# First two 256-row slots of a mixture-of-experts kernel joined into one of 512 rows

## The reference

```
h = rmsnorm(layernorm(x)) * gamma
q, kv, a = split(h @ w_qkva.T);  a = sigmoid(a)
y[n] = a[n] * y[n-1] + kv[n]            # scan along the 1024 rows of a batch
x = x + q * y
z = layernorm(x)
logits = z @ router_w.T                 # 7 experts, the best 2 taken
combine = softmax over the 2 best logits, placed at their experts
x = x + sum_e combine_e * swiglu_e(z) + swiglu_shared(z)
swiglu(z) = (silu(z @ wg) * (z @ wu)) @ wd        # 256 -> 1024 -> 256
```

## Time and profile before

| | us |
|---|---|
| median of 3 runs (982.82 to 985.39) | 982.82 |
| the profiled execution's own time | 982.58 |
| its span | 980.8 |
| PE busy in the span | 972.9 (99%) |
| DVE busy | 587.6 (60%) |
| ACT busy | 477.4 (49%) |
| POOL busy | 395.3 (40%) |

### The profile page before, as it was taken

How to read it: one execution, slowest core, us unless ns; L and a number is a source line. 1 busy time by engine, 2 the same in 40 slices (tenths; PEclk the granted TensorE clock), 3 DMA queues, 4 the chain that set the end, 5 groups by cost and what they waited for, 6 DMA issues and landing times.

```text
span 980.8 us, 15883 instructions
## 1 busy us (share of the span) xinstructions
PE 972.9 (99%) x5565; PEld 849.2 (87%) x5565; DVE 587.6 (60%) x1043; ACT 477.4 (49%) x769; POOL 395.3 (40%) x265
## 2 busy tenths in 40 slices
PE   8999999999999999999999999999999999999998
PEld 6888998888889998888888888888888999999887
DVE  7988687787653134455445544654464455646677
ACT  5565434323422324456545544554465466767564
POOL 3336100000021243464645554655556488776300
PEclk9999999999999999999999999999999999999999
DMA  9433300000049995544463456345535576775393
GB/s 320 120 87 86 87 22 22 16 8 22 1 139 356 326 297 181 199 123 145 166 207 102 158 175 202 94 164 183 189 89 176 188 266 209 267 240 166 89 331 107
DMA packets 146034, 155.06 MB, mean 158 GB/s; under 512 B 75449, under 2 KB 134338, under 8 KB 138818
## 3 DMA queue, kind: packets, MB, share of 16 engines
q1 hardware_dynamic: 139248, 136.08, 42.8%
q0 software_dynamic: 6720, 18.36, 6.0%
q10 hardware_dynamic: 18, 0.01, 0.0%
HBM read 127.67 MB, written 26.74 MB: 157 GB/s over the span
## 4 chain that ended last, share of the span: by engine, by line
PE 93%; DVE 4%; ACT 1%; issue 1%; POOL 0%; DVEq 0%; POOLq 0%; ACTq 0%
PE ps L1158 40%; PE ps L1136 15%; PE ps L1114 11%; PE ps L1139 8%; PE ps L1020 6%; PE ps L1204 4%; PE ps L1181 4%; PE ps L1212 2%; PE ps L1002 1%; PE ps L1031 1%; DVE h_lo L1767 1%; PE ps L983 1%; DVE h_early L1761 1%; ACT h_hi L886 1%; DVE y_sb L1354 0%
## 5 line engine op out<-in xcount | busy, mean ns | idle before, releaser
L1158 PE MATMUL ps<-xs_hi,w_both 128*128 128x512 f32 x1216 | 380.4, 391 | 0.1
L1158 PEld LDWEIGHTS ps<-xs_hi,w_both 128*128 128x128 f32 x1216 | 228.3, 188 | 49.0 <-DVE ps L1761 0.9
L652 POOL TENSOR_TENSOR w_both<-w_raw,w_both 128x2048 fp32r<-128x2048 f32 x45 | 223.5, 4966 | 107.1 <-ACT w_both L823 98.5
L1158 PE MATMUL ps<-xs_lo,w_both 128*128 128x512 f32 x608 | 236.7, 389 | 0.0
L1136 PE MATMUL ps<-w_both,h_hi 128*128 128x512 f32 x656 | 233.0, 398 | 0.1
L1139 PE MATMUL ps<-w_both,h_lo 128*128 128x256 f32 x656 | 184.1, 281 | 0.0
L1767 DVE TENSOR_TENSOR h_lo<-ps,h_hi 128x512 fp32r<-128x512 f32 x152 | 105.1, 691 | 103.1 <-ACT h_hi L886 81.7
L676 POOL DMA_INDIRECT x_stage<-z_rows,idx_x x70 | 72.3, 1032 | 224.8 <-DVE idx_x L1673 160.8
L1761 DVE TENSOR_TENSOR ps<-ps,silu 128x512 f32<-128x512 f32 x152 | 106.2, 699 | 90.8 <-ACT silu L879 62.2
L879 ACT ACTIVATE silu<-ps 128x512 f32<-128x512 f32 x152 | 90.7, 597 | 134.9 <-PE ps L1158 134.6
L1136 PEld LDWEIGHTS ps<-w_both,h_hi 128*128 128x128 f32 x656 | 123.3, 188 | 30.2 <-DVE h_lo L1767 0.4
(11 more groups left out here) (229 smaller groups left out, 1080.1 us busy)
## 6 DMA issues: line engine op xcount, KB each, us to landing
w_raw<-in_L_ffn_w_gate_dram SPq DMA_DIRECT2D x20, 1024.0 KB, 4.9
w_raw<-in_L_ffn_w_up_dram SPq DMA_DIRECT2D x20, 1024.0 KB, 7.0
w_raw<-in_L_ffn_w_down_dram SPq DMA_DIRECT2D x20, 1024.0 KB, 5.8
sorted_rows<-x_stage SPq DMA_DIRECT2D x32, 256.0 KB, 2.2
x_rows<-sorted_rows SPq DMA_DIRECT2D x128, 64.0 KB, 2.0
w_spare<-in_L_ffn_w_up_dram SPq DMA_DIRECT2D x6, 1024.0 KB, 5.6
w_spare<-in_L_ffn_w_gate_dram SPq DMA_DIRECT2D x6, 1024.0 KB, 8.7
w_spare<-in_L_ffn_w_down_dram SPq DMA_DIRECT2D x6, 1024.0 KB, 11.5
```

The source lines that it names most:

```text
L652: pool.tensor_tensor(w_lo[buf][:, k, :], w_raw[buf][:, k, :], w_hi[buf][:, k, :].bitcast(F32), ALU.subtract).then_inc(wlo_ready[k], 1)
L1158: last = pe.matmul(ps[:, 2 * (j % 2) + part, :], w[:, part, kd * H + j * P:kd * H + (j + 1) * P], xx[:, h // 2, kd, :], start=i == 0, stop ...
```

## The change

Slots 0 and 1 become one quad on all three engines. Unit 0 is turned and split in group 5 and unit 1 in group 6 (`UNIT_AT`), each with `x_lo` between the halves of the scan; group 7 has no such work left. On ACT the `x_hi` of these units stands ahead of `h_rows` and `h_hi_part` of its group. PE waits for the splits in `turn_back`. SP loads units 2 and 3 ahead of the store of z of group 7. ACT normalizes the last group two tiles at a time, behind steps 2 and 3, and copies the turned z behind step 4. On PE `last_back` stands ahead of block 0, the logits of group 5 ahead of block 2, those of group 6 and `turn_last_z` (now into banks 4 and 5) ahead of block 5, the logits of group 7 ahead of block 7, `ranks` behind the third row tile. On DVE `logits_and_z` stands behind step 3 (of 8), the logits of group 6 behind step 5, `choices` behind step 7; `rank_totals`, `rank_blocks` and `rank_quarters` follow the first addition, `rank_kinds` the second; `places` goes behind step 0 of quad 2, `pair_targets` from step 0 to 3 and `lone_places` from 3 to 5.

```diff
+        UNIT_AT = {NC - 3: 0, NC - 2: 1}
@@ SP
+            for n in (2, 3):
+                load_x(n, n, z_dram, n % 2)
             store_z(NC - 1)
             sp.wait_ge(z_out[NC - 1], 16)
-            for n in range(2, SA):
+            for n in range(4, SA):
                 load_x(n, n, z_dram, n % 2)
@@ ACT
+            def last_z_rows(t0, t1):
+                act.wait_ge(scaled2, NC)
+                for t in range((NC - 1) * CT + t0, (NC - 1) * CT + t1):
+                    last = act.activation(z_all[:, t, :], resid[:, t, :], ACT.Identity,
+                                          scale=scale2[:, t:t + 1], bias=bias2[:, t:t + 1])
+                if t1 == CT:
+                    last.then_inc(z_ready, 1)
...
-                elif g < NC - 2:
-                    h_rows(g + 2)
+                else:
+                    if g in UNIT_AT:
+                        x_hi(UNIT_AT[g], UNIT_AT[g])
+                    if g < NC - 2:
+                        h_rows(g + 2)
                 if g + 1 < NC:
                     h_hi_part(g + 1)
-                else:
-                    x_hi(0, 0)
...
-            slot(0, 0, early=True, turns=((2, 1),), between={1: lambda: z_rows(NC - 1), 2: zT_copy})
-            slot(1, 1, early=True, turns=((1, 1), (3, 2)))
+            quad(0, 0, early=True, between={2: lambda: last_z_rows(0, 2), 3: lambda: last_z_rows(2, CT), 4: zT_copy})
@@ PE
             def turn_last_z():
                 pe.wait_ge(z_ready, NC)
-                pe.wait_ge(gated, 5)
+                pe.wait_ge(res_ready, NC)
...
+                if g in UNIT_AT:
+                    pe.wait_ge(x_split, UNIT_AT[g] + 1)
...
+                    if t == ST and JH + 1 in between:
+                        between[JH + 1]()
...
-            slot(0, 0, 0, between={0: last_back, 2: lambda: last_routes(NC - 3),
-                                   6: lambda: last_routes(NC - 2), JH - 1: turn_last_z},
-                 down=lambda: last_routes(NC - 1), skip=0)
-            slot(1, 1, 0, between={1: ranks}, skip=0)
+            quad(0, 0, 0, skip=0, wide=False, between={
+                0: last_back, 2: lambda: last_routes(NC - 3),
+                5: lambda: (last_routes(NC - 2), turn_last_z()), 7: lambda: last_routes(NC - 1), JH + 1: ranks})
@@ DVE
-                if g == NC - 1:
-                    turn_x(0, LD)
-                scan(g, None if g + 1 < NC else lambda: x_lo(1, 0))
+                if g in UNIT_AT:
+                    n = UNIT_AT[g]
+                    turn_x(n, LD)
+                    scan(g, lambda: x_lo(n + 1, n))
+                else:
+                    scan(g)
...
-            slot(0, 0, turns=((1, 1, loads(1)),), shared=0, early=True, skip=0, between={
-                ("gated", 0): lambda: statistics2(NC - 1), 1: logits_and_z,
-                2: lambda: take_logits(NC - 2, 7), "down": choices})
-            slot(1, 1, turns=((0, 1, loads(2)), (2, 2, loads(3))), shared=1, early=True, skip=0, between={
-                0: rank_totals, 1: rank_blocks, 2: rank_quarters, "down": kinds_and_places})
+            def totals_and_blocks():
+                rank_totals()
+                rank_blocks()
+                rank_quarters()
...
+            quad(0, 0, turns=ahead_of(0), shared=0, early=True, skip=0, between={
+                ("gated", 0): lambda: statistics2(NC - 1), 3: logits_and_z, 5: lambda: take_logits(NC - 2, 7),
+                "down": choices, "half": totals_and_blocks})
+            rank_kinds()
             betweens = {
-                2: {0: pair_targets, 3: lone_places, 6: lone_targets, 7: find_pairs, "down": move_all,
+                2: {0: places, 3: pair_targets, 5: lone_places, 6: lone_targets, 7: find_pairs,
+                    "down": move_all,
```

More of the change, by code:

```diff
@@ L785, in zT_copy @@
                 act.wait_ge(zT_ready, NC - 1)
-                act.activation(zT[NC - 1][:, :, :], ps[:, 0:2, :], ACT.Copy).then_inc(zT_ready, 1)
+                act.activation(zT[NC - 1][:, :, :], ps[:, 4:6, :], ACT.Copy).then_inc(zT_ready, 1)
             prepare(0, PARTS[0])
@@ L992, in turn_last_z @@
                         z = z_all[:, (NC - 1) * CT + k, :].rearrange("p (i k) -> p k i", k=KD)
-                        last = pe.transpose(ps[:, kd, k * P:(k + 1) * P], z[:, kd], ident[:, :])
+                        last = pe.transpose(ps[:, 4 + kd, k * P:(k + 1) * P], z[:, kd], ident[:, :])
                 last.then_inc(zT_psum, 1)
@@ L1812, in quad @@
                     gate(n, j, par, early, skip, ps[:, 2 * par + 1, :].rearrange("p (j n) -> p j n", j=2))
+                    if ("gated", j) in between:
+                        between["gated", j]()
                     rest(n, j, par, early, skip, h_lo[:, j, :].rearrange("p (j n) -> p j n", j=2),
@@ L1868, in logits_and_z @@
                 turn_z(NC - 2)
-            def kinds_and_places():
-                rank_kinds()
-                places()
             def move_all():
```

## The result

| | before | changed |
|---|---|---|
| median of 6 runs, us | 983.22 | 992.31 |
| range, us | 982.82 to 985.39 | 991.47 to 993.82 |
| profiled execution, us (span) | 982.58 (980.8) | 991.47 (989.7) |

Ratio 1.0091, 95% interval 1.0080 to 1.0102: slower by 9.1 us, where the forecast time of 986.9 (range 984.2 to 988.9) is 3.7 above this median of the kernel before. The direction was right and the time lies outside the range.

The account below looks back on a forecast made before the run. The prediction took PE to bound the kernel, DVE next. Matmul savings of -1.27 and -0.3 us against added waits summed to +4.12 on 982.58, about 986.9 with the median's 0.24; range 984.2 to 988.9.

Parts of the forecast that it names:

- What bounds the kernel: Whole kernel: PE is the bound, so a change is worth its matmul time less new waits for DVE or ACT.
- Matmul time: Joined slots 0 and 1: 512-column matmuls replace 256-column ones, -1.27 us; a stall in slot 1 goes, -0.3.
- Groups 5 and 6: `x_lo` between the scan's halves delays the starts of groups 6 and 7 by 0.59 us each, +1.17 for the two.
- Rival 2: The turnings in groups 5 and 6 are hidden, all else as forecast: 985.5 us, chance 0.13.
- `last_back` ahead of block 0: Group 7's turning back, with no block ahead, waits for `times_q`: 1.53 us lost against 0.46 before, +1.07.
- Block 5: Logits of group 6: a 4.3 us chain under 2.72 of matmuls, and ACT 0.7 late: +2.3 us, the largest term.
- Block 7, `ranks`, quad 2: PE waits for group 7's logits, +0.35 us; for `ranks`, +0.1; for the last `rest` in quad 2's down part, +0.7.
- Quad 4: The quad after quad 2 starts with 1 us and more to spare on DVE, so no added time.
- rival 4: The clock falls in the 2.3 us wait ahead of the logits of group 6; chance 0.03.

Follow-up runs that it names:

- e6: e1 with `x_hi` behind the rounding of the next group's rows and `x_lo` behind `h_lo_part` in groups 5 and 6: 984.71 us, ratio 1.0009.
- e1: Changed kernel with group 6's logits and the turning of the last z ahead of block 6 instead of 5, ACT's copy one step later: 985.82 us.
- e2: Changed kernel with 10 spare 512-column matmuls, result unused, in the wait ahead of the logits of group 6: 989.15 us, ratio 1.0054.
- e10: Changed kernel with 2 spare 512-column matmuls, result unused, in the 0.43 us wait ahead of the logits of group 7: 990.36 us.
- e5: Changed kernel with group 7 turned back behind block 0 of the quad instead of ahead of it, plus a wait for group 4's logits: 991.55 us.
- e9: Changed kernel with 5 spare 512-column matmuls, result unused, in the 2.37 us wait ahead of the logits of group 6: 992.18 us.
- e3: Kernel before the change with z of group 6 turned one step later on DVE and its logits copied behind step 3: 995.85 us, ratio 1.0123.
- e8: e6 with group 7 turned back behind block 0 and `lone_targets` moved behind step 7 of quad 2: 982.58 us, ratio 0.9990.

## Why the prediction was right in direction and wrong in size

*What bounds the kernel*: right. Every one of the forecast waits of PE came, at its place, and was still there at the end.

*Matmul time*, -1.27 and -0.3: right, -1.42 measured; two matmuls of 256 columns at the pitch of 0.120 take 0.013 more than one of 512 at 0.2268, and 96 times that carried it. One reading in it was off: quad 4 began at 175.84, not at 175.90, so quad 2 took 33.18 and a tile of its first form 2.83. The two tiles in the other form (2.88) then cost 0.1 more, which puts the forecast at -1.47.

*Groups 5 and 6*: right, +1.17 both ways, and the place of the work is the reason: e6 gave back 1.1 by moving `x_lo` out of the scan, and `x_hi` on ACT behind the rounding, with the same work on both. It moved the two together, so their shares aren't parted. Rival 2 is out.

*`last_back` ahead of block 0*: right mechanism, 1.75 lost instead of 1.53. `times_q` ended at 102.40 and PE went at 102.65; I had allowed the 0.06 us of the kernel before (101.30 to 101.36). Why it took 0.25 here isn't shown: ahead of block 5 it is 0.26 too, but ahead of groups 6 and 7, where PE also stood idle, 0.05.

*Block 5*: right, 2.37 for 2.3, with silu of step 3 (117.14) 0.6 late behind the rows of group 7; the chain from it to the turned z took 4.01 in both kernels. *Block 7, `ranks`, quad 2*: right within 0.15. *Quad 4*, "1 us and more to spare on DVE": wrong by 0.38. All kernels with the joined slots have that wait, at one place (DVE idle 0.57 us behind `hot_val`, 0.21 before, with its silu done well ahead both times). I didn't find out why.

*The step that failed is rival 4, the clock*, with a chance of 0.03 and left out of the sum: it came, twice, for 3.4 of the 4.8 us that are missing. No row of the kernel before shows what a fall costs; measured were 1.7 for each stretch, in which the pitch of 512-column matmuls was 0.43 beside 0.2268. e1, e2 and e10 show that it is what the time went to. In the executions at a mean clock of 0.995 it came to one stretch more. What failed was the evidence against it: between 0 and 4 us PE is busy for only 0.60 us and the granted clock is shown as 1.00. That 1.00 isn't the clock of those first matmuls. In the changed kernel's timeline, the first turnings and later ones of the same shape:

```profile
3.41 3.25 PE L961 MATMUL ps<-ident 128*128 128x128 f32 x14 [3.41 <-POOL lane L620]
...
85.73 1.03 PE L996 MATMUL ps<-ident,z_all 128*128 128x128 f32 x8
```

By their starts the 14 are 0.213 apart and the 8 are 0.109 apart, and the kernel before has the same two pitches (0.213 up to 6.0 us, 0.109 from 7.1 on). The eight turnings behind the logits in e5, where the granted clock is shown as 0.50, are 0.213 apart as well (from 123.07 to 124.35). So by its pitch PE began at the lower clock, while the window from 0 to 10 us is shown with 1.00 like the earlier trace rows. Here the pitch of matmuls of one form tells the clock where the column doesn't. With it, PE would have been seen to be slow behind its first wait of 3.4 us, the evidence against the rival would have been gone, and its chance and the range (by another 3.4 us) should have been larger. How short a wait is enough, no row of the kernel before could tell: behind the start the longest in its list of PE's waits is 0.3. In the runs, waits of 2.2 us, and of 0.93 in e9, were enough with small matmuls behind them.

## What to carry to other kernels

A wait of PE with small matmuls behind it cost here its length and then 1.7 us for each stretch at a granted clock of 0.50: price both, or put wide matmuls there (3.2 us less in e2). Where an operation on DVE is moved by a step, count the chain from the end of the block that starts it to the matmul that needs it, and compare with the matmul time between; 4.3 against 2.72, with 0.7 for what ACT does first, gave the wait to 0.1 us. Read the clock from the pitch of equal matmuls (0.213 against 0.109 here) before using it as evidence, and look at the mean clock of every execution: the profile may be of one with fewer falls than the median has.

## What the runs showed of the hardware

- A wait of 1.59 us, with 0.8 us of turnings and then wide matmuls behind it, left the granted clock at 1.00. Behind one of 0.93 ahead of 16 matmuls of 7 columns and 8 turnings it was 0.50, from 2.3 us after the wait on. Behind waits of 2.2 us this took 1.9 us in the changed kernel and 0.5 in e5; in a wait of 3.7 us (e3) the clock fell before the wait was over. Ten wide matmuls of unused result (2.3 us) in a wait were worth 3.2 us.
- A fall cost 1.7 us each time in the changed kernel's profile, 3.4 for the first in e5, where it came early in the logits.
- The first wide matmul of group 0 starts at 10.45 us in the profile before and at 10.59 to 11.14 in those of the kernels made from the changed one, waiting for DVE by up to 0.53 us. It goes with the moment from which the trace records the full clock, ahead of which the turnings have the longer pitch (0.213 instead of 0.109): 6.1 us in the profile before, 6.4 in e8 (10.59), 7.3 in the changed kernel (10.76), 9.5 in e6 (11.14). Profiles of kernels that are alike up to there differ by some tenths for it.
